# A gated linear attention block: when VectorE takes its statistics, scans and early splits, and where TensorE waits

## The reference

```python
x = x + attention(layernorm(x), Wq, Wk, Wv, Wo, Wa, ba)
x = x + (layernorm(x) @ CB.T) * (SCB / 127) + bias
# attention: q = elu(x@Wq)+1, k = elu(x@Wk)+1, v = x@Wv, a = sigmoid(x@Wa + ba + 2)
# per head and token:  S = a*S + k v^T;  z = a*z + k;  out = (q.S) / (q.z + 1e-6);  then out @ Wo
```

## Time and profile before

| | us |
|---|---|
| median of 3 runs | 2191.49 (2190.68 to 2196.81) |
| profiled execution | 2204.02 |
| its span, first to last instruction | 2202.2 |
| TensorE busy | 2064.2 (94%) |
| VectorE, ScalarE, GpSimd busy | 1497.7 (68%), 677.4 (31%), 340.1 (15%) |

### The profile page before, as it was taken

One profiled execution on the slowest core, in us unless ns is written; L12 is line 12 of the kernel. 1 busy time (PEld: TensorE's weight loads), 2 busy tenths in 40 slices (PEclk: granted clock), 3 DMA queues, 4 the chain that ended last, 5 costly groups with the idle time before them and its releaser, 6 DMA issues. The chain is left out here.

```text
span 2202.2 us, 71551 instructions
## 1 busy us (share of the span) xinstructions
PE 2064.2 (94%) x28424; PEld 1773.7 (81%) x28424; DVE 1497.7 (68%) x3308; ACT 677.4 (31%) x1288; POOL 340.1 (15%) x367
## 2 busy tenths in 40 slices
PE   4789999999999999999999999999889999999998
PEld 3677888888888888888888888888768888888887
DVE  5566767777767777777776777776755555555555
ACT  3333333333333333333333333333321111111111
POOL 1111122111113111112211112211000000000000
PEclk8899999999999999999999999999999999999999
DMA  5132332333332333333233333324423333333332
GB/s 178 43 95 84 96 96 82 87 98 113 94 94 86 86 91 107 100 96 91 86 85 105 108 91 96 86 82 131 124 99 114 114 114 111 113 114 111 111 110 88
DMA packets 204592, 220.81 MB, mean 100 GB/s; under 512 B 31360, under 2 KB 146560, under 8 KB 204544
## 3 DMA queue, kind: packets, MB, share of 16 engines
q1 hardware_dynamic: 204544, 220.13, 32.7%
HBM read 168.59 MB, written 51.44 MB: 100 GB/s over the span
## 5 line engine op out<-in xcount | busy, mean ns | idle before, releaser
L1189 PE MATMUL G<-w_hi,xT_hi 128*128 128x512 f32 x1024 | 414.2, 404 | 55.2 <-DVE xT_lo L817 39.2
L1189 PE MATMUL G<-w_lo,xT_hi 128*128 128x512 f32 x1024 | 404.0, 395 | 0.0
L1189 PE MATMUL G<-w_hi,xT_lo 128*128 128x512 f32 x1024 | 401.9, 392 | 0.0
L1189 PE MATMUL G<-xT_hi,w_hi 128*128 128x256 f32 x1024 | 292.0, 285 | 8.3 <-DVE w_lo L824 8.3
L1189 PE MATMUL G<-xT_hi,w_lo 128*128 128x256 f32 x1024 | 292.0, 285 | 0.0
L1189 PE MATMUL G<-xT_lo,w_hi 128*128 128x256 f32 x1024 | 291.9, 285 | 0.0
L681 ACT ACTIVATE relu_t<-G 128x512 f32<-128x512 f32 x256 | 152.8, 597 | 450.7 <-PE G L1189 450.7
L1189 PEld LDWEIGHTS G<-w_hi,xT_hi 128*128 128x128 f32 x1024 | 194.6, 190 | 109.5 <-issue 68.5
L906 DVE SCALAR_TENSOR_TENSOR qT<-exp_t,relu_t 128x512 f32<-128x512 f32 x128 | 88.9, 695 | 257.3 <-ACT exp_t L682 257.3
L1189 PEld LDWEIGHTS G<-w_hi,xT_lo 128*128 128x128 f32 x1024 | 194.6, 190 | 42.8
L1189 PEld LDWEIGHTS G<-w_lo,xT_hi 128*128 128x128 f32 x1024 | 195.0, 190 | 35.3
(11 more groups left out here) (131 smaller groups left out, 3757.2 us busy)
## 6 DMA issues: line engine op xcount, KB each, us to landing
abc<-decay_rows SPq DMA_DIRECT2D x256, 128.0 KB, 3.0
pbc<-product_rows SPq DMA_DIRECT2D x256, 128.0 KB, 3.1
attn_rows<-attn SPq DMA_DIRECT2D x512, 64.0 KB, 2.0
at_rows<-attn_rows SPq DMA_DIRECT2D x64, 512.0 KB, 3.3
xt<-in_x SPq DMA_DIRECT2D x64, 256.0 KB, 2.7
x_in<-in_x SPq DMA_DIRECT2D x64, 256.0 KB, 3.4
out_rows<-xt SPq DMA_DIRECT2D x64, 256.0 KB, 2.0
xT_in<-in_xT SPq DMA_DIRECT2D x31, 512.0 KB
```

What stands on the lines that cost most here:

```text
L1189: made = nc.tensor.matmul(to, lhs, rhs, start=(n == 0), stop=(n == len(passes) - 1))
```

## The change

ScalarE: `split_hi(1)` comes before step -1, the others one place earlier; `x_hi(0)` comes before `copy_num(0)` and the exponential of the logits. VectorE: `x_lo(0)` before `decays`; `decay_matrix(0)` before `elu_q(1)` (odd) and before `elu_q(3)` and `elu_k(0)` (even); the statistics of a pair move from the even step to the end of the odd step before (for the first pairs: the end of step 0). TensorE: the waits of the block, but for those named in the diff, stand in front of `transposes`; `scores(1)` and `scores(0)` share one wait; at the start `gate_logits` follows k0's unit. SP and GpSimd are unchanged.

```diff
@@ scalar
             for s in range(2):
                 first_x_hi(s)
+            split_hi(1)
...
                 if exists(i - 2):
                     copy_num(1)
+                if gates and not first:
+                    act.wait_ge(xT_normal, pairs[0])
+                    act.wait_ge(v_unit_ready[1], one[-1])
+                    act.wait_ge(q_unit_ready[3], pairs[0])
+                    x_hi(0)
                 if exists(i - 1):
                     copy_num(0)
-                if b == 1 and exists(i + 1):
+                if second:
+                    split_hi(4)
+                if gates and not first:
                     exp_logits()
@@ vector
-                normal = b == 0 and exists(i + 2)
+                normal = b == 1 and exists(i + 3) and not first
...
-                if gates:
+                if gates and not first:
+                    x_lo(0, pairs[1], xT_in[:, :, tokens(0)])
                     decays()
-                    if not first:
-                        x_lo(0, pairs[1], xT_in[:, :, tokens(0)])
-                if normal:
-                    x_stats(x16[1])
...
                     elu_q(0, 0)
                     if first:
-                        split_lo(2)
+                        split_lo(3)
+                    decay_matrix(0)
+                    if normal:
+                        x_stats(x16[2])
+                        dve.wait_ge(stats_ready, pairs[2])
+                        dve.wait_ge(norm_stored, x16[0])
                     elu_q(1, 1)
+                    if normal:
+                        x_moments(pairs[2])
                 elif exists(i + 1):
+                    elu_q(2, 1)
+                    decay_matrix(0)
                     if second:
-                        split_lo(5)
-                    elu_q(2, 1)
+                        x_stats(x16[1])
+                        dve.wait_ge(stats_ready, pairs[1])
                     elu_q(3, 0)
+                    if second:
+                        x_moments(pairs[1])
                     elu_k(0, 1)
-                if exists(i + 1):
-                    decay_matrix(0)
@@ tensor, transposes()
+                    for r in range(2):
+                        if exists(i - 1 - r):
+                            pe.wait_ge(M_ready[r], one[-1 - r])
+                            pe.wait_ge(qs_ready[r], one[-1 - r])
+                            pe.wait_ge(mid_ready[r], one[-1 - r])
                     if exists(i - 1):
+                        pe.wait_ge(vw_ready[1], one[-1])
+                        pe.wait_ge(state_ready[0], one[-1])
+                        wait(pe, num_copied[0], one[-2])
+                        if b == 0 and exists(i + 1):
+                            pe.wait_ge(logits_ready, pairs[0])
+                        for u in range(2, 4):
+                            pe.wait_ge(q_ready[u], pairs[-1] if b == 0 else pairs[0])
                         pe.wait_ge(k_ready[1], one[-1])
-                        wait(pe, M_ready[1], one[-2])
                     if exists(i):
-                        wait(pe, M_ready[0], one[-1])
+                        pe.wait_ge(q_ready[0], pairs[0])
                         pe.wait_ge(k_ready[0], count)
@@ tensor, scores()
+                    count = due("scores", one[0])
+                    if exists(i):
+                        pe.wait_ge(q_ready[1], pairs[0])
+                    pe.wait_ge(kT_copied[0], one[0])
+                    pe.wait_ge(kT_copied[1], count)
+                    begin("scores")
                     for r in (1, 0):
                         if exists(i - r):
-                            count = due(f"scores{r}", one[0])
-                            for u in range(2 * r, 2 * r + 2):
-                                pe.wait_ge(q_ready[u], pairs[-1] if r == 1 and b == 0 else pairs[0])
-                            pe.wait_ge(kT_copied[0], one[0])
-                            pe.wait_ge(kT_copied[1], count)
-                            begin(f"scores{r}")
```

More of the change, by code:

```diff
@@ L728, in step @@
                     copy_kT()
+                gates = b == 1 and exists(i + 1)
                 if exists(i - 2):
                     copy_num(1)
+                if gates and not first:
[3 more added lines that the diff above has]
+                    x_hi(0)
                 if exists(i - 1):
                     copy_num(0)
-                if b == 1 and exists(i + 1):
+                if second:
+                    split_hi(4)
+                if gates and not first:
                     exp_logits()
-                    if not first:
[L736 to L741, removed]
                 if exists(i):
@@ L744, in step @@
                     if second:
-                        split_hi(4)
+                        split_hi(5)
                     copy_v(1)
-                if b == 1:
-                    if exists(i + 1):
[L749 to L762, removed]
+                if gates:
+                    if not first:
+                        x_hi(1)
+                    k0_parts()
+                    if first:
+                        split_hi(2)
+                        exp_logits()
+                    q_parts(0)
+                    if first:
+                        split_hi(3)
+                    chunk_decay()
+                    q_parts(1)
+                    copy_v(0)
+                elif b == 1 and exists(i):
+                    chunk_decay()
+                    rows_hi(1, 0)
                 elif exists(i):
-                    if second:
-                        split_hi(5)
                     q_parts(2)
@@ L888, in step @@
                 one = counts(dve, i, 1, (-3, -2, -1, 0, 1))
-                pairs = counts(dve, pair, 1, (-1, 0, 1))
-                x16 = counts(dve, pair, 16, (-1, 1))
+                pairs = counts(dve, pair, 1, (-1, 0, 1, 2))
+                x16 = counts(dve, pair, 16, (-1, 0, 1, 2))
                 c32 = counts(dve, i, 32, (-1, 0, 1))
@@ L1021, in step @@
                         scaled_q(r)
-                if gates:
+                if gates and not first:
+                    x_lo(0, pairs[1], xT_in[:, :, tokens(0)])
                     decays()
-                    if not first:
-                        x_lo(0, pairs[1], xT_in[:, :, tokens(0)])
-                if normal:
-                    x_stats(x16[1])
                 if exists(i - 1):
-                    if normal:
-                        dve.wait_ge(stats_ready, pairs[1])
-                        wait(dve, norm_stored, x16[-1])
                     normalised(0)
[L1033 to L1036, removed]
                 if isinstance(i, int) and i == NC - 1:
@@ L1039, in step @@
                 if second:
-                    split_lo(3)
+                    split_lo(4)
                 if exists(i):
                     elu_k(1, 0)
-                    if second:
-                        split_lo(4)
                     if gates:
@@ L1051, in step @@
                     if first:
-                        split_lo(1)
+                        logit_sums()
+                        split_lo(2)
+                        decays()
                     elu_q(0, 0)
                     if first:
-                        split_lo(2)
+                        split_lo(3)
[4 more added lines that the diff above has]
+                        dve.wait_ge(norm_stored, x16[0])
                     elu_q(1, 1)
+                    if normal:
+                        x_moments(pairs[2])
                 elif exists(i + 1):
+                    elu_q(2, 1)
+                    decay_matrix(0)
                     if second:
-                        split_lo(5)
-                    elu_q(2, 1)
+                        x_stats(x16[1])
+                        dve.wait_ge(stats_ready, pairs[1])
                     elu_q(3, 0)
+                    if second:
+                        x_moments(pairs[1])
                     elu_k(0, 1)
-                if exists(i + 1):
-                    decay_matrix(0)
                 if isinstance(i, int) and i == NC - 3:
@@ L1155, in output_product @@
                     made.then_inc(Y_ready, 1)
[L1157 to L1162, removed]
+            first_due = {"k transposed": FIRST + 1, "within1": FIRST - 1, "scores": FIRST + 1, "carried": FIRST - 1,
+                         "delta": FIRST + 1, "gates": FIRST // 2 + 1, "within0": FIRST}
             due_of = {stage: pe.alloc_register(stage.replace(" ", "_") + "_due") for stage in first_due}
@@ L1237, in carried @@
                 def carried(r):
[L1239 to L1246, removed]
+                    if not (exists(i) or exists(i - 1)):
+                        pe.wait_ge(M_ready[r], one[-1 - r])
+                        pe.wait_ge(qs_ready[r], one[-1 - r])
+                        pe.wait_ge(mid_ready[r], one[-1 - r])
+                        pe.wait_ge(num_copied[0], one[-2])
+                    if r == 0 and exists(i - 2):
```

(13 more changed lines are left out.)

8 lines of the change are left out of this document (5 added, 3 removed).

## The result

The changed kernel takes 2290.9 us (median of 4 runs, 2286.6 to 2293.2) against 2191.1 us: 1.0447 times as long, interval 1.0422 to 1.0471. It is slower, as forecast, and by twice what was forecast (+49.9 us on the sum, +99.8 measured), outside the range.

What follows compares the result with a forecast made beforehand. TensorE was taken as the bound, busy 94% of the span. Late rows in the pairs +60, last odd step -2 and start -9 sum to +49 us: 2191.5 to 2241 us, range 2185 to 2280.

Steps and rivals of the forecast that it cites:

- Rows late by SP's queue: Odd step's end: bn_stats waits for xt rows, sent last in SP's queue; 2222 to 2262 us, chance 0.66.
- rows in time: Rival, odd step's end: the second xt lands early enough, a pair takes 45.7 us; 2130 us, chance 0.17.
- The chain: One pair from the odd block's start: 4.7 to the gates, 8.4 to aT cleared, 36.3 to the next: 49.4 us.
- From the second bn_stats to delta(0): VectorE's odd tail into the even block: from 14.7 us to 18.25 us after aT is cleared.
- The clock: Start of the kernel: some 5 us more at 1.2 GHz after a new wait for xT_in.
- Landing and bn_stats: Odd step's end: rows landed 14.0 us after aT is cleared, second bn_stats at 14.7.
- the gates: Odd block: gate logits start 4.7 us after the block's start, between 4.35 and 5.2.
- a case inside the range: Scan gone from beside GpSimd's passes: both end sooner, gates start at 4.35, a pair takes 49.05 us.
- How many pairs pay: 2.0 us more a pair in the 30 odd steps with a pair to come (1 to 59): +60 us.
- The start: First 83 us: most of 24.4 us of w_lo waits goes, less 8 of new wait and 5 of clock: -9.
- Early waits: Front of TensorE's blocks: taken as hidden, 0 us; if exposed, 0.5 us a block, +32, chance 0.11.
- The last odd steps: End of the scan: the last full odd step has no statistics and keeps its gain, -2 us.

Runs made afterwards that it cites:

- Undoing part 2: Changed kernel with the statistics put back in the even step, all else as changed: 2137.5 us, 0.9759 of the kernel before.
- Turning the loop: Changed kernel with VectorE's loop body cut as odd step then even step, so the jump back lies ahead of an odd step: 2248.9 us, 1.0259.
- part 2 alone: Kernel before with only the statistics moved to the odd step's end, the scan still last, step 0's statistics unmoved: 2335.7 us, 1.0635.

## Why the prediction was right in kind and wrong in size

**The cause stands.** Rows late by SP's queue: moving the loads alone gives back 129 us. The rival *rows in time* had said 45.7 us a pair and 2130 us. Its own case, rows early and the statistics at the odd end, takes 46.42 us a pair and 2159.9 us, for it had no term for the loop's turn and for step 0's late statistics either; without these two it is 45.94 and 2140.5. Undoing part 2 gives 45.79 and 2137.5.

**The chain.** In the pair at 1191.95, from the odd block's start: gates 4.24 (forecast 4.7), aT cleared 12.64 (13.1), the second bn_stats done 14.88 later (14.7), delta(0) 4.45 after that (3.55), k1's unit 1.10 (1.10), next odd block 16.90 (16.92): 49.97 us, forecast 49.4. The steps that failed are two terms that the sum put at nothing: the loop's turn on VectorE, measured at 0.87 us a pair, and the lower clock behind the stalls, 1.0 to 1.2 us a pair. Term by term:

1. *From the second bn_stats to delta(0)*: I summed the busy times of elu_q(1), moments, vw and state(1), and missed the 0.87 us ahead of vw. Turning the loop removes it and takes 0.74 us out of this term (3.71). So it is the loop's turn, and the same gap with early rows shows that the rows don't make it. The list of waits of before has no such row; there the scan stood last in the body, ahead of weighted_v(0), and with part 2 alone, where it still does, the gap isn't seen either. +0.9 us a pair.
2. *The clock.* I gave it 5 us at the start and nothing in the pairs, where I forecast stalls of over 3 us in sum in each. +1.0 to 1.2 us a pair, 27 to 30 us in the 26 pairs.
3. *Landing and bn_stats*: +0.15 to 0.2. Against these *the gates*: 4.24 and not 4.7, -0.45. Between 240 and 1620 us the gates wait for GpSimd once. Here the rule of the Trainium skill ("SBUF — State Buffer", Who interferes with whom) that I had set beside the sum is borne out: the scan moved away from GpSimd's passes takes 1.22 us, and took 1.89 beside them; GpSimd's first pass took 4.5 us on average in these pairs and takes 3.9 now. I had noted it as a case inside the range, with the gates at 4.35, and took the other.
4. *How many pairs pay*: I put the 2.0 us on 30 odd ends. The loss is in the 26 pairs from step 7 on; bn_stats waits at the ends of steps 1, 3 and 5 too, but the five steps from step 2 on and the pair from step 59 on are 0.5 us longer in all. What hides it there was not looked for. With 2.0 us on 26 pairs the term is 52 and not 60, so by luck this miss took 8 us off the other two.

49.4 + 0.9 + 0.2 - 0.45 is 50.05; the nine pairs in which the half clock is over by delta(0) take 50.07 on average; with the 1.2 of the clock it is the 51.23 of all 26.

**The start**: -18.1 us at step 2's block, forecast -9, at the edge of my 0 to 18. The splits alone give -20.8: of the 24.4 us of waiting for w_lo 2.5 are left. The price of step 0's late statistics is there, in its place: TensorE waits 6.3 us for xT_in ahead of step 1's gates (forecast 8), and step 1 takes 31.0 us, 6.65 more than with early statistics. Not forecast: waits of 7.2 us for kT, 1.6 before. Summed over the start, TensorE's waits are 28.4 us now and 40.2 before, some 12 us less; the rest of the gain is the clock, which I had put in with the wrong sign, as 5 us of cost:

```profile
0.00:89.54 89.54, 61.19 (x616) 52.26 (x617) 52.18 (x111) 33.47 (x65) 11.96 (x29) 0.92 0.40 125
```

The mean granted clock to step 2's block is 0.92; in the kernel before it was 0.86 to that block (0 to 107.66 us). So TensorE stood at the half clock for 13.7 us and not 30.7.

**Early waits**: 0 forecast, +3.6 us alone, from the last steps. **The last odd steps**: -2 forecast; from step 61's block on it is +3.1, of which the front waits make 2.6 in step 63; the last full odd step, 61, gains 0.7.

In the sum: pairs +97.6 and not +60, start -18.1 and not -9, the end +3.1 and not -2. That gives +82.6 and not +49. The own range of the forecast, 2222 to 2262, had no term for either of the two that failed.

## What to carry to other kernels

Before work is moved earlier on one engine, ask for the semaphore count that it will read and find the instruction on the other queue that raises it; here it was the last item of SP's step, and one line's place in that queue was worth 129 us. Price a new stall on TensorE twice, for the time it stands and for the lower clock after it, and add the loop's own turn to the price of a late instruction at the end of a loop's body. When a gain vanishes, read who waits first on the next engine: the pbc wait on ScalarE was covered until the odd half had become shorter, and then it was worth 32 us.

## What was unexpected of the hardware

- A stall of 2.3 us ahead of scores with 0.7 to 1.6 us ahead of delta(0) brought TensorE to 1.2 GHz in every pair; whether that cost nothing or 1.8 us depended on how far the half clock reached past the stalls. Ten spare products of 512 columns in the first of the stalls removed it in 21 of 26 pairs.
- The turn of the loop costs VectorE 0.87 us when short instructions stand last in the body, as late rows (22.7 us in 26 turns) and early rows (22.7 in 26) both show. The compare and branch itself takes 0.056 us; 0.26 us pass from its end to the next instruction, and five instructions on registers take another 0.49. With a scan of 1.22 us standing last, none of it shows.
- A VectorE scan takes 1.22 us with GpSimd idle and 1.88 beside its two passes (means of 52 and of 25 scans in the trace of before).
